# Dealing the pieces of a row-maxima pass over the slots of a software-pipelined attention stage

## The reference

```python
q, k = apply_rotary(q), apply_rotary(k)          # 16 heads of 64
logits = einsum('bhqd,bhkd->bhqk', q, k)
logits = where(causal, logits, -1e9) / sqrt(64)
out = einsum('bhqk,bhkd->bhqd', softmax(logits), v)
```

## Time and profile before

| | |
|---|---|
| median of 3 runs | 2807.57 us (2807.42 to 2808.52) |
| the profiled execution, its own time | 2809.57 us |
| span of its trace, first to last instruction | 2807.8 us |
| PE busy | 2678.8 us, 95% |
| DVE busy | 2081.0 us, 74% |
| ACT busy | 1827.2 us, 65% |
| POOL busy | 628.8 us, 22% |
| mean granted TensorE clock | 0.987 of full speed |

### The profile page before, as it was taken

One profiled execution on the slowest core, in us unless ns is written; L12 is line 12 of the kernel. 1 busy time (PEld: TensorE's weight loads), 2 busy tenths in 40 slices (PEclk: granted clock), 3 DMA queues, 4 the chain that ended last, 5 costly groups with the idle time before them and its releaser, 6 DMA issues. The chain is left out here.

```text
span 2807.8 us, 50126 instructions
## 1 busy us (share of the span) xinstructions
PE 2678.8 (95%) x19664; PEld 1468.5 (52%) x19664; DVE 2081.0 (74%) x3515; ACT 1827.2 (65%) x2499; POOL 628.8 (22%) x414
## 2 busy tenths in 40 slices
PE   5999999979999999889979999999999999999997
PEld 2444444468888888755534444444444444444443
DVE  7975666568777877556657887878888887887785
ACT  4713334369999999942247767676767667776766
POOL 0100000058888888821120000000000000000006
PEclk9999999999999999999989999999999999999999
DMA  4452322221112212222211121111111111111125
GB/s 161 116 187 90 90 76 83 57 80 43 44 51 55 55 34 54 73 76 90 90 53 53 46 53 53 48 51 53 53 47 52 52 47 53 53 50 51 50 76 202
DMA packets 83907, 196.67 MB, mean 70 GB/s; under 512 B 13280, under 2 KB 17760, under 8 KB 83424
## 3 DMA queue, kind: packets, MB, share of 16 engines
q1 hardware_dynamic: 83680, 193.58, 23.3%
HBM read 157.81 MB, written 35.72 MB: 69 GB/s over the span
## 5 line engine op out<-in xcount | busy, mean ns | idle before, releaser
L587 ACT ACTIVATE shared<-shared,offsets 128x512 f32<-128x512 f32 x992 | 658.9, 713 | 85.8 <-DVE shared L616 45.9
L1083 POOL TENSOR_TENSOR shared<-shared 128x1024 f16<-128x1024 f32 (+1 forms) x256 | 523.0, 2072 | 116.7 <-ACT shared L1218 107.8
L1661 PE MATMUL gp<-region,ring 128*128 128x512 f16 x2112 | 461.5, 380 | 4.6 <-DVEq L1806 3.1
L1682 PE MATMUL yp<-wo_ahead,shared 128*128 128x512 f16 x2016 | 450.6, 381 | 15.9 <-DVE wo_ahead L634 5.5
L329 DVE TENSOR_REDUCE maxima<-sx 128x1 f32<-128x512 f32 (+3 forms) x640 | 362.8, 603 | 96.3 <-PE sx L319 63.8
L1661 PE MATMUL gp<-region,head 128*128 128x512 f16 x1920 | 416.8, 379 | 0.0
L616 DVE TENSOR_TENSOR shared<-shared 128x512 f32<-128x512 f32 x496 | 341.3, 688 | 28.2 <-DVE shared L616 0.5
L1213 ACT ACTIVATE shared<-st,coef 128x1024 f16<-128x1024 f32 (+1 forms) x320 | 321.2, 1004 | 46.0 <-PE st L1146 39.8
L384 POOL TENSOR_TENSOR maxima<-maxima,eps 128x1 f32<-128x1 f32 x48 | 9.2, 191 | 1499.7 <-ACT shared L1783 1314.1
L915 PE MATMUL pq<-region,ht 128*128 128x512 f16 x1536 | 339.8, 380 | 3.0 <-DVEq L969 3.0
L1661 PEld LDWEIGHTS gp<-region,ring 128*128 128x128 f16 x2112 | 207.1, 98 | 256.1 <-issue 6.8
(11 more groups left out here) (164 smaller groups left out, 3898.9 us busy)
## 6 DMA issues: line engine op xcount, KB each, us to landing
qk_pairs<-r_pair SPq DMA_DIRECT2D x128, 128.0 KB, 2.3
shared<-in_down_codes SPq DMA_DIRECT2D x42, 256.0 KB, 3.0
shared<-in_down_scales SPq DMA_DIRECT2D x84, 128.0 KB, 3.3
shared<-in_gate_codes SPq DMA_DIRECT2D x40, 256.0 KB, 3.1
shared<-in_gate_scales SPq DMA_DIRECT2D x80, 128.0 KB, 3.3
shared<-in_up_codes SPq DMA_DIRECT2D x40, 256.0 KB, 3.1
shared<-in_up_scales SPq DMA_DIRECT2D x80, 128.0 KB, 3.3
xt<-in_x SPq DMA_DIRECT2D x16, 512.0 KB, 5.6
```

Of the source, the lines that this page charges most:

```text
L587: a.activation(line[:, k % 4, :], code7, ACT.Identity, scale=slope, bias=offsets[:, k:k + 1]).then_inc(s_L.sem, 1)
L1083: eng.tensor_tensor(pt_pair[:, n0(u, g) % PT_RING, 1, 0:w], probs[:, n0(u, g) % P_RING, 0:w], pt_pair[:, n0(u, g) % PT_RING, 0, 0:w], ALU. ...
L1661: mm = pe.matmul(gp[:, e % 2, m, :], wgu[par][:, m, a, col0:col0 + P], xnT[:, b, k, tok], start=(k == 0 and a == b), stop=(k == KT - 1 and ...
L1682: mm = pe.matmul(yp[:, d % 4, :], inter[:, c % 2, a, t, j * P:(j + 1) * P], wd[:, b, t * E + n * CH:t * E + (n + 1) * CH], start=(t == 0 a ...
```

## The change

The even deal of pieces is taken away. For heads 3 to 15 a list by group, MAXIMA_AT, says how many pieces a slot gets. It is rotated so that it begins with the group at which such a head starts, and the pieces are dealt out in their old order.

```diff
-        per_slot = [[] for _ in range(NGH)]
-        for k in range(NI):
-            per_slot[k * NGH // NI].append(k)
...
         assert sum(FIRST_SLOTS) == sum(SECOND_SLOTS) == NI
+        MAXIMA_AT = [1, 3, 3, 2, 3, 3, 2, 1, 1, 3, 2, 3, 3, 1, 1, 2, 3, 1, 1, 1]
+        first_group = (2 + len(FIRST_SLOTS) + len(SECOND_SLOTS)) % NGH
+        by_slot = MAXIMA_AT[first_group:] + MAXIMA_AT[:first_group]
+        assert len(by_slot) == NGH and sum(by_slot) == NI
...
-            counts = {1: FIRST_SLOTS, 2: SECOND_SLOTS}.get(head, [len(p) for p in per_slot])
+            counts = {1: FIRST_SLOTS, 2: SECOND_SLOTS}.get(head, by_slot)
```

## The result

The kernel with the new deal takes 2828.13 us (2827.72 to 2829.53), against 2808.05 (2807.42 to 2808.99) for the kernel before on the same chip: slower, ratio 1.0073, 95% interval 1.0061 to 1.0085, 20.1 us. The forecast was 2829.7, range 2818 to 2842.

What follows compares the result with a forecast made beforehand. The prediction took TensorE with its waits as the bound; removed waits of 2.33 us against 3.17, 0.39 and 0.5 added gave + 1.73 us a head, + 22 us in thirteen heads, hence 2829.7 us, range 2818 to 2842.

Steps and rivals of the forecast that it cites:

- The bound: Heads 3 to 15: nothing but TensorE can bound a whole head, busy 37.58 of 39.19 us; the rest are its waits.
- Removed waits: TensorE's waits for VectorE maxima and for ScalarE, largest behind groups 7 and 17: all 2.33 us a head go.
- The third piece: Slots of three in groups 1, 2, 4, 5, 9, 11, 16: the last piece waits for a bank, adding 3.17 us a head.
- The round trip: Time from a slot's first piece to its third, which waits for the first one's maximum with two banks: 1.17 us.
- piece a: First piece of a slot of three, issued together with the second, before half of the products with V.
- The turn: Group 12: the second piece waits until VectorE has read the previous head's turned maxima from its bank, adding 0.39 us.
- The low half of group 19: VectorE's low half, held by GpSimd, delays maxima so group 1's third piece is late: 0.5 us a head, bounds 0 and 0.7.
- The sum: - 2.33 + 3.17 + 0.39 + 0.5 = + 1.73 us a head, + 22 us over thirteen heads.
- The faster one: Rival: waits go and the third piece is hidden; with no wait there, 25 us less, 2782 us; chance 0.06.
- The third rival: VectorE falls behind, late low halves cost 0.7 us also in groups 2 and 9: 38 us longer, 2845; chance 0.09.
- c: Third piece of a slot of three, issued after half of the products; with two banks it waits for the first piece's maximum.
- The signs: Trace marks of being right: head about 40.9 us, third piece 1.17 us behind first, maxima waits 3.6 to 4.3 a head.

Runs made afterwards that it cites:

- the first: Changed kernel, but in slots of three in heads 3 to 15 one piece stands ahead of the products, one between their halves, one behind: 2797.85 us, ratio 0.9963.
- the second: Changed kernel, but in heads 3 to 15 VectorE takes the maximum over only the first half of a piece's columns: 2803.19 us, ratio 0.9982.
- the fourth: Changed kernel, with group 12's three pieces alone put one ahead of the products, one between their halves and one behind: 2822.32 us, ratio 1.0052.
- the run with one part undone: Changed kernel, with two pieces each in groups 16 and 18 in place of three and one: 2828.9 us, ratio 1.0076.

## Why the prediction was right

**The bound.** TensorE with its waits makes the head, before and after. The twenty slots of a head, each its work and its waits, add up to the head's 40.78 us, and the runs that changed only waits (the first, the second and the fourth) moved the time by what they took away.

**Removed waits, taken as 2.33 us a head.** The waits behind groups 7 and 17 did go: the first piece of group 9 follows its scores at once, slot 19 has 0.06 us of wait in place of 0.89, and the run with one part undone brings that one back. The term was a little too small. The added waits sum to 3.23 + 0.39 + 0.57 = 4.19 us, the head grew by 1.60, so 2.6 were removed. Of the missing 0.27, slots 2 and 17 of before explain about 0.2 (each was some 0.1 longer than its work, short waits that I had not counted); the rest is within the rounding of so many slots.

**The third piece, 3.17 us.** Measured 3.23, slot by slot within 0.02. The round trip of 1.17 us, read in two heads that the change did not touch, held in the thirteen others. For a piece a of 384 columns it was 1.03, as taken (groups 11 and 16). The first two experiments show that it is this and not the fullness of the wide slots.

**The turn, 0.39 us.** The fourth experiment gave 0.37 a head.

**The low half of group 19, taken as 0.5 between 0 and 0.7.** 0.57 by the slot, 0.56 by undoing one part. The bounds were worked out; the 0.5 between them was a choice. The order of events that was followed is the one that the trace shows: low half, maximum, output, maximum of a. That GpSimd's operation holds it is read from the timing: 104 ends at 0.40 to 0.43 us behind GpSimd's, and 0.55 us for a low half with none beside it. No run took GpSimd's operation away.

**The sum.** + 1.73 us a head against + 1.60, + 22 us against + 20.8 in the stretch and 20.1 by the medians. The forecast was too high mainly because the gain was taken too small; the third piece and the low half, each 0.06 or 0.07 too small as well, made up for part of it.

**The rivals.** The faster one decided at a round trip of 0.99 us. With the maximum shortened to 0.42 us the round trip was 0.90, and that kernel was indeed faster than the one before, by 0.18%. The point of the change was sound on that side; it was the round trip through two banks that made it a loss. No run had a third bank. The third rival would have had late low halves in groups 2 and 9 too; their slots have 0.61 and 0.44 us, the plain round trip. Its sum was wrong too: with 0.7 us in three groups it comes to 3.3 us a head and not 2.9, some 2851 us. The Trainium skill's rule on rotating banks (page "Perfetto Trace Analysis", section "Matmuls") would have made a gain of it. The traces agree with it only as far as there is enough work between two uses of a bank: with the pieces spread, c doesn't wait in groups 4, 5, 9 and 11; with a and b together it does.

**The signs.** One head took 40.78 us where about 40.9 was said, and the waits of maxima pieces for maxima rose to 3.8 us a head, within the 3.6 to 4.3. In each slot of three c does start 1.17 us behind a, except where a has 384 columns (1.03), in group 1 (1.73) and in group 12 (1.20).

**What the prediction missed** was not a number but a question: it took the place of c in the slot as given. Moving it costs nothing and turns + 20 us into - 10.

## What to carry to other kernels

With two buffers between two engines, three items close together cost the round trip less the work that lies between the first and the last of them (only two buffers were tried here); count that for each slot before the items are dealt out by the slots' room. Read the round trip from a place of the trace where it already occurs and nothing else is queued on the other engine. Then spread the items within the slot: the same deal was 20 us slower than the even one in one order and 10 us faster in another.

## What the runs showed of the hardware that was not expected

VectorE's low half ends 0.40 to 0.43 us behind the end of the GpSimd operation that is under way, 52 times of 52 in the changed stretch before and after, and takes 0.55 us alone. So its duration tells when GpSimd ended and not how much work it is. One other number was sharper than expected: the distance from a piece to the next use of its bank was 1.17 us in heads 1 and 2 of the kernel before and in heads 3 to 15 of the changed one, with different operands and other engines' loads beside it, and 0.90 with a maximum of 256 columns.
